# Two attention layers with 16 heads: row maxima turned by VectorE and through memory, the transposed input read from memory, scores 12 instead of 16 iterations behind the maxima, and a finer order table

## The reference, cut to what matters

```python
x = _layernorm(x + _L0_attn_ref(x, w_qkv, w_proj))                  # self: q, k rotated
x = _layernorm(x + _L0_xattn_ref(x, ctx, ctx, Wq, bq, Wk, ...))     # cross: keys, values of ctx
x = _layernorm(x + _L0_ffn_ref(x, ...))                             # windows of 128, 8 heads; MLP; twice

# self and cross, 16 heads of 16 features each, B = 8, S = 512:
attn = softmax(einsum('bhqd,bhkd->bhqk', q, k) * scale)
out = einsum('bhqk,bhkd->bhqd', attn, v) ... @ w_proj (+ bo)
```

## Time and profile before

| | |
|---|---|
| median of 3 runs | 2249.5 us (2247.09 to 2249.76) |
| span of the profiled execution | 2234.3 us, mean granted TensorE clock 0.972 |
| PE busy | 2109.7 us (94%) |
| DVE, ACT, POOL busy | 1661.7 (74%), 1501.9 (67%), 1327.5 us (59%) |
| 16-head part: first maximum to last score | 43 to 981 us |

### The profile page before, as it was taken

How to read it: one execution, slowest core, us unless ns; L and a number is a source line. 1 busy time by engine, 2 the same in 40 slices (tenths; PEclk the granted TensorE clock), 3 DMA queues, 4 the chain that set the end, 5 groups by cost and what they waited for, 6 DMA issues and landing times.

```text
span 2234.3 us, 44819 instructions
## 1 busy us (share of the span) xinstructions
PE 2109.7 (94%) x13992; PEld 1475.9 (66%) x13992; DVE 1661.7 (74%) x3987; ACT 1501.9 (67%) x3418; POOL 1327.5 (59%) x1376
## 2 busy tenths in 40 slices
PE   3899999999999999977999999899989999998998
PEld 2544444444444444346888888788878888887887
DVE  4777888777888888747888888656388888886675
ACT  2287777777888888855777777554367777775443
POOL 0344555533334444477888877454378887875775
PEclk7699999999999999999999999999999999999999
DMA  7667677665756666434545455300055554552111
GB/s 154 109 125 147 140 146 137 144 143 124 154 136 155 159 160 137 140 101 105 131 109 115 103 115 110 93 26 6 1 138 116 111 113 107 108 114 62 58 62 43
DMA packets 201337, 248.92 MB, mean 111 GB/s; under 512 B 26584, under 2 KB 119512, under 8 KB 201112
## 3 DMA queue, kind: packets, MB, share of 16 engines
q1 hardware_dynamic: 198552, 237.68, 47.7%
q0 software_dynamic: 2560, 8.39, 1.1%
HBM read 97.47 MB, written 63.44 MB: 72 GB/s over the span
## 4 chain that ended last, share of the span: by engine, by line
PE 77%; DMA 5%; POOL 5%; SPq 4%; ACT 3%; DVE 3%; issue 2%; POOLq 0%; ACTq 0%; DVEq 0%
PE PS L485 14%; PE PS L487 12%; PE PS L486 12%; PE PS L606 9%; PE PS L590 8%; PE PS L573 5%; PE PS L699 5%; PE PS L675 5%; PE PS L684 4%; DMA KS<-hs 3%; PE PS L659 2%; SPq L1496 2%; SPq L1464 1%; ACT PT L827 1%; DMA hs<-HL 1%
## 5 line engine op out<-in xcount | busy, mean ns | idle before, releaser
L1003 DVE TENSOR_REDUCE MX<-PS 128x1 f32<-128x512 f32 x1024 | 642.5, 682 | 167.1 <-PE PS L573 156.9
L827 ACT ACTIVATE PT<-PS 128x512 f32<-128x512 f32 x1024 | 546.2, 599 | 129.5 <-PE PS L590 127.6
L573 PE MATMUL PS<-KS,QS 48*128 48x512 f32 x1024 | 357.0, 454 | 43.7 <-DMA KS<-hs 33.5
L590 PE MATMUL PS<-QS,KS 50*128 50x512 f32 x1024 | 385.5, 456 | 6.4 <-ACT PT L827 6.0
L590 PEld LDWEIGHTS PS<-QS,KS 50*128 50x128 f32 x1024 | 164.9, 187 | 270.5 <-issue 212.3
L1369 POOL TENSOR_TENSOR PB<-PB,RC 128x512 f32<-128x512 f32 (+1 forms) x256 | 250.6, 999 | 48.6 <-DVE RC L1123 48.6
L606 PE MATMUL PS<-PT,VP 128*17 128x512 f32 x2048 | 273.6, 606 | 2.9 <-ACT OT L834 2.9
L890 ACT ACTIVATE PB<-PB,NMf 128x256 f32<-128x256 f32 (+1 forms) x512 | 242.6, 478 | 8.6 <-DVE NMf L1114 8.5
L573 PEld LDWEIGHTS PS<-KS,QS 48*128 48x128 f32 x1024 | 171.5, 192 | 108.0 <-issue 59.3
L1349 POOL TENSOR_TENSOR RI<-RI,mhalf 128x8 f32<-128x8 f32 x128 | 214.1, 1672 | 10.7
L1114 DVE CUSTOM_DVE_ANT_0 PB<-PS,mk 128x256 f32<-128x256 f32 (+1 forms) x512 | 175.7, 385 | 54.4 <-PE PS L675 54.2
(11 more groups left out here) (182 smaller groups left out, 5054.4 us busy)
## 6 DMA issues: line engine op xcount, KB each, us to landing
qT<-QN SPq DMA_DIRECT2D x384, 128.0 KB, 2.4
hs<-HL SPq DMA_DIRECT2D x64, 512.0 KB, 3.8
kT<-kT SPq DMA_DIRECT2D x256, 128.0 KB, 2.5
QS<-hs SPq DMA_DIRECT2D x192, 128.0 KB, 5.9
KS<-hs SPq DMA_DIRECT2D x192, 128.0 KB, 8.0
od<-OT SPq DMA_DIRECT2D x64, 256.0 KB, 5.9
OC<-od SPq DMA_DIRECT2D x32, 256.0 KB
cst<-rs SPq DMA_DIRECT2D x32, 256.0 KB
```

The costliest lines, as they stand in the source:

```text
L573: pe.matmul(PS[:, bank, :], QS[rows, s, h // 2, qt * P:(qt + 1) * P], KS[rows, s, h // 2, :], start=True, stop=True).then_inc(fills("amax" ...
L590: pe.matmul(PS[:, bank, :], KS[rows, s, pair, kt * P:(kt + 1) * P], QS[rows, s, pair, :], start=True, stop=True).then_inc(fills("score", v ...
L827: act.activation(PT[:, kt % 2, 2 * i + half], PS[:, TURNS["score", vb, g, kt, half, i][0], :], ACT.Exp).then_inc(drains("score", vb, g, kt ...
L1003: dve.tensor_reduce(MX[:, vb % 2, h // 8, qt, c:c + 1], PS[:, TURNS["amax", vb, h, qt][0], :], AX, ALU.max).then_inc(drains("amax", vb, h, ...
```

## The change

Five things change together, all in the 16-head part.
1. The maxima no longer pass TensorE and ScalarE. GpSimd splits them as before; VectorE turns 32 x 32 blocks (`maxturn`, MT<-MB, 128 x 64 in one instruction); SyncE writes them to memory (`max_out`, two transfers of 128 rows of 32 numbers) and reads them back into the score operand (`max_in`, two transfers). The sign goes into the constant rows of KS, which are -1 now.
2. For the self batches the transposed input is an array of its own in memory (x_T, made when the inputs are laid out). SyncE loads it (`load_xt`, 512 KB) into the place of the low half, ScalarE casts the high half (`xt_hi`), GpSimd makes the low half (`xt_lo`). The untransposed X is still loaded, later. `tr` is left for the cross batches only.
3. Scores run LAG = 12 iterations behind the maxima instead of 16, over the borders of the steps.
4. The tables have 96 places a step instead of 32 slots, six an iteration, and other places and lags for nearly every stage; LAST_STEP moves by 24 slots in number, which is the same distance from the end.
5. `stats` waits for the `norm` that used its buffer last, since the new order doesn't give that by itself.

```diff
+LAG = 12
 SELF_ORDER = (
-    (1, "stats", (1,), 4), (1, "ot", (3,), 2), (1, "spread", (), 3), ...
+    (0, "xt_hi", (1,), -1), (2, "mix_sum", (0, 0), -1), (3, "maxturn", (1,), 1), (3, "out_lo", (1,), 3), (4, "ot_out", (3,), 2),
...
-    for step in range(min(lags), NV + 1):
-        a, b = step, step - 1
-        at = [[] for _ in range(32)]
+    for n in range(16 * min(lags), 16 * NV + LAG + 1):
+        for half in range(2):
+            slot = 2 * n + half
             for i in range(2):
-                both = [("score", b, g, k, half, i), ("amax", a, 4 * g + 2 * i + 1 - half, k)]
+                a, b = n, n - LAG
+                both = [("score", b // 16, b // 4 % 4, b % 4, half, i), ("amax", a // 16, 4 * (a // 4 % 4) + 2 * i + 1 - half, a % 4)]
                 out += [s for s in (both if half == 0 else both[::-1]) if 0 <= s[1] < NV]
+                out += places.pop(3 * slot + i, ())
+            if half and 0 <= n - LAG - 1 < 16 * NV:
+                p = n - LAG - 1
+                out.append(("pv", p // 16, p // 4 % 4, p % 4))
+            out += places.pop(3 * slot + 2, ())
...
-            def maxtr(vb, half):
-                pe.wait_ge(sem["max_parts"], 2 * (2 * vb + half + 1))
-                bank = vacant(pe, "maxtr", vb, half)
-                for qt in range(4):
-                    m = pe.transpose(PS[0:16, bank, qt * P:(qt + 1) * P], f(MB[:, half, qt]).rearrange("p a h -> p (a h)"), ident[:])
-                m.then_inc(fills("maxtr", vb, half), 1)
-            def negmax(vb, half):
-                act.wait_ge(*filled("maxtr", vb, half))
...
+            def xt_hi(vb, kc):
+                act.wait_ge(sem["xt_in"], 16 * (vb + 1))
+                act.copy(xT[:, kc, 0], xT0[:, kc, 1]).then_inc(sem["x_hi"], 1)
+            def maxturn(vb, half):
+                dve.wait_ge(sem["max_parts"], 2 * (2 * vb + half + 1))
+                if vb:
+                    dve.wait_ge(sem["max_out"], 32 * (2 * vb + half - 1))
+                dve.transpose(MT[:, half].rearrange("p k c -> p (k c)"), f(MB[:, half]).rearrange("p k c -> p (k c)")).then_inc(sem["max_turned"], 1)
+            def xt_lo(vb, kc):
+                pool.wait_ge(sem["x_hi"], n_xhi(vb, kc))
+                pool.tensor_tensor(xT[:, kc, 1], xT0[:, kc, 1], f(xT[:, kc, 0]), ALU.subtract).then_inc(sem["x_lo"], 1)
+            def load_xt(vb):
+                if vb:
+                    sp.wait_ge(*filled("val", vb - 1, 1))
+                sp.dma_start(xT0[:, :, 1], t["x_T"][:, vb * S:(vb + 1) * S].rearrange("(k p) s -> p k s", p=P)).then_inc(sem["xt_in"], 16)
+            def max_out(vb, half):
+                sp.wait_ge(sem["max_turned"], 2 * vb + half + 1)
+                if vb:
+                    sp.wait_ge(sem["max_in"], 32 * (2 * vb + half - 1))
+                for k in range(2):
+                    v = t["ms"][half, k].rearrange("x (b j) -> b x j", b=4)
+                    sp.dma_start(v, MT[:, half, k]).then_inc(sem["max_out"], 16)
+            def max_in(vb, half):
+                sp.wait_ge(sem["max_out"], 32 * (2 * vb + half + 1))
+                if vb >= 2:
+                    sp.wait_ge(*filled("score", vb - 2, 2 * half + 1, 3, 1, 1))
+                for k in range(2):
+                    v = t["ms"][half, k].rearrange("(r c t) i -> r c (t i)", r=2, c=4)
+                    sp.dma_start(f(QS[48 + k:P:64, vb % 2, 4 * half:4 * half + 4]), v).then_inc(sem["max_in"], 16)
```

More of the change, by code:

```diff
@@ L153 @@
+            out += places.pop(3 * slot + 2, ())
+    for place in sorted(places):
+        out += places[place]
+    return out
 WINDOW_ORDER = (
@@ L595, in pv @@
                     if vb == 0:
[L596 removed]
+                        pe.wait_ge(sem["pv_zero"], 1)
                         pe.wait_ge(sem["ones_v"], 1)
```

215 lines of the change are left out of this document (103 added, 112 removed).

## The result

The changed kernel takes **2284.7 us** (median of 4 runs, 2284.3 to 2285.3) where the kernel before takes 2248.3: a ratio of **1.0173** with a 95% interval of 1.0152 to 1.0194. That is 36 us slower by the medians and 39 by the ratio, which is not formed from the medians. The forecast was 2242, with a range of 2212 to 2268. The profiled executions stand at 2283.1 us (span) against 2234.3: 48.8 us more. They are 12 more than the medians show, because the profiled execution of the kernel before was a quick one: in every other run the launch takes some 2 us more than the span of the same execution, so this one took about 2236.5, where the median is 2248.3. The 15 us between median and span, which the text before the result puts down to the launch, are mostly this.

The account below looks back on a forecast made before the run. TensorE, busy 54.3 or 54.4 of a 55.0 us steady step, was taken as the bound. Terms: -51 + 15 (start) + 20 (input) + 9 (reciprocal) = -7 against 2249.5, forecast 2242 us, range 2212 to 2268.

Parts of the forecast that it names:

- The size of the gain: 16-head part: fewer transposes, four fewer iterations and no TensorE waits for GpSimd at the maxima gain 51 us.
- the four iterations fewer: End of the 16-head part: lag 12 shortens it from 272 to 268 iterations, gaining 10.3 us.
- its 31 us: TensorE's transposes removed: 2.9 us less per self batch, 1.2 per cross batch, 31 us in all.
- the input of batch 1: Start: its load, queued on SyncE behind the first stack and X loads, lands near 62.
- C: Rival, slower: the same VectorE and ScalarE waits, each with the lower clock's price; +16, 2265 us; chance 0.27.
- the wait for the sums in steps 6 to 9: VectorE's reciprocal waits 1.9 us for the sums there, without input on GpSimd; covered, so costed at nothing.
- What one wait costs TensorE: Steps 2 to 5: VectorE's 4.5 us wait for the sums, 2.9 covered, costs TensorE 1.6, plus 0.7 low clock.
- The clock: Low TensorE clock after waits: 1 us a step beside the input's wait, 0.7 beside the sums' wait.
- The input of batches 2 to 7: Steps 0 to 5: ScalarE's cast waits 4 to 5.5 us for its load behind the stack; 20 us, bounds 0 and 33.
- The start: Step 0: batch 1's first projection comes 11 us later, plus about 4 at low clock; 15 us, bounds 3 and 20.
- D: Rival, late maxima: second-half scores wait for the maxima's way through memory; +10 to +30 us; chance 0.06.

Follow-up runs that it names:

- g1: f2 with the transposed input loaded at place 5 (before 60) and the residual at 6 (before 38): 2201.9 us, ratio 0.9793.
- g2: g1 with the context's load of the cross batches at place 34 (before 45): 2186.4 us, ratio 0.9736.
- e1: Changed kernel with the load of the sums at place 24, in front of the second stack, instead of 33: 2249.5 us, ratio 1.0023.
- e3: Changed kernel with the transposed input's load issued by ScalarE at place 79 instead of SyncE at 86: 2278.7 us, ratio 1.0188.
- f1: Changed kernel with the raw transposed input in a place of its own, loaded from place 60, residual loaded afterwards: 2277.5 us, ratio 1.0149.
- e2: Changed kernel with VectorE's reciprocal at place 44 (before 32), its write and spread also 12 places later: 2262.8 us, ratio 1.0114.
- f2: Changed kernel with both f1's early raw input and e1's sums in front of the second stack: 2232.3 us, ratio 0.9953.
- e4: Changed kernel with the start's X, identity and bias loads issued behind batch 1's transposed input: 2286.7 us, ratio 1.0224.
- f3: f2 with cross-batch places moved: reciprocal's spread 48 to 36, context 45 to 62, one heads' write 49 to 51: 2241.4 us, ratio 0.9999.

## Why the prediction was wrong

The forecast was a gain of 7 us, the profile shows a loss of 48.8: 56 us off. By stretch the forecast was too low by 36.5 us in steps 1 to 9, 9 in step 0, 8.5 in steps 10 to 14 and 2.5 behind them. In its terms:

*What held.* The size of the gain: an undisturbed cross step took 53.0 (forecast 53.8), a self step 52.5 in g1 and g2 (52.1); the four iterations fewer gave 9.0 with the transposes of the last step (forecast 10.3 + 1.2). The gain of steps 1 to 9 was even larger than its 31 us: undisturbed they take some 474 us (below), 40 less than before, as the waits for the stack went too (8.3 us of TensorE before, which the sum doesn't have). The waits and their places: the input of batch 1 landed at 61.0 (forecast near 62), in step 4 VectorE came to the reciprocal 18.9 us into the step (it begins at 299.3) and the sums landed 24.3 into it (19.1 and 23.6), and TensorE stood where the text says. C, the same waits each with the clock's price, was the nearest rival and was given 0.27; its 2265 us were still 20 too low, as it has no wait for the sums in steps 6 to 9 either.

*The step that failed: the wait for the sums in steps 6 to 9.* "...in steps 6 to 9 there is no input on GpSimd, the wait is 1.9 and covered." VectorE waited 4.9, 6.0, 5.1 and 9.3 us there, and TensorE 3.4, 5.6, 4.8 and 9.0: 22.8 of its 33 us stand in steps that were costed at nothing. The sum took GpSimd's 2.6 us for the input off the chain. At most 1.1 us of them were on it. In step 4, which has this work ahead of it, VectorE turned the maxima 3.5 us into the step after waiting 1.06 us for GpSimd; in step 7, which hasn't, it did so 3.8 us into the step without a wait, as work of its own came first. SyncE's queue in the two steps (step 7 begins at 478.8):

```profile
303.11 1.14 SPq L1529 DMA_DIRECT2D ms<-MT  x2
305.67 1.04 SPq L1537 DMA_DIRECT2D QS<-ms  x2
306.89 2.66 SPq L1511 DMA_DIRECT2D QS<-hs  x6
```
```profile
482.82 1.14 SPq L1529 DMA_DIRECT2D ms<-MT  x2
485.38 1.03 SPq L1537 DMA_DIRECT2D QS<-ms  x2
486.59 2.68 SPq L1511 DMA_DIRECT2D QS<-hs  x6
```

The stack begins 7.6 and 7.8 us into the step (forecast 8.4 and 5.8), and the sums land at 24.3 in both. In step 9 the stack begins at 11.5 only, as SyncE waits for the heads' write first.

*What one wait costs TensorE* was mis-sized by a smaller amount, 1.6 us where steps 2 to 5 show 1.2, 1.8, 3.9 and 3.2. The cover was right: from VectorE's stop to TensorE's it is 2.8 us in steps 2 to 6 (forecast 2.9), where all four banks were free and a projection stands between the maxima. In steps 7 to 9, where the banks still held two maxima and no projection stands there, it is 1.55. What the sum lacks is the way back: when the sums have landed, the reciprocal and the first reduction must pass before a bank is free, 324.84 - 323.60 = 1.24 us, in all eight steps. With it the terms close: 41.6 + 8 x 1.24 - 5 x 2.77 - 3 x 1.55 = 33.0 us. Step 7, VectorE and TensorE, for 5.96 + 1.24 - 1.55 = 5.65:

```profile
503.08 0.55 DVE L1016 RECIPROCAL RR<-RT 128x64 f32<-128x64 f32 x1 [5.96 <-DMA RT<-od]
```
```profile
504.32 0.76 PE L578 MATMUL PS<-KS,QS 48*128 48x512 f32 x1 [5.64 <-DVE MX L999]
```

e1 shows the worth of this term by a run: 35 us, though part of what the waits gave back went to others.

*The clock.* I put 1 and 0.7 us beside a wait, some 8 in all. Steps 1 to 9 are 548.5 us; at 52.5 and 53.0 they would be 6 x 52.5 + 3 x 53.0 = 474. Of the 74.5 more, 46.7 are the idle time of TensorE and 28 are left for the lower clock: 0.6 us for each us waited. This is an estimate by subtraction; the mean granted clock of the 548.5 us, 0.91, fits it: some 98 us of them stood at the lower level, idle time included. The rows for it were there before the change (a wait of 2.4 us in steps that grew by 4.5 and 6.0), and rival C used them; the forecast should have.

*The input of batches 2 to 7: the right size from a wrong cause.* Costed at 20 us, measured 12.0 of TensorE and its share of the clock. ScalarE's wait was 0.3 to 5.2 us where I had 4 to 5.5, but TensorE waited as long as ScalarE, where I took off 1.4: the cast and the first exponential, which come before a score bank is free, used up the cover. The cause I gave, the stack ahead in the queue, doesn't explain it: e3 took the queue away and the wait grew, f1 took the buffer's gate away, issued the load 26 places earlier and it was gone, while the load took the same 7.7 us in both.

*The start:* +15 forecast, less 2.9 for the transposes, and +21 measured. The first projection of batch 1 came at 64.23 (forecast 65; before 54.91, forecast 54). TensorE waited 17.9 us for it, and then 3.2 for ScalarE, where it waits for its next input, and 1.1 for the maxima's rows; before, its waits in this step were some 3 us. The mean granted clock of the step was 0.61 and not 0.66. How the rest divides between clock and waits was not tried.

*D, given 0.06,* cost the changed kernel some 8 us: steps 10 to 14 took 277.0 where five of 53.8 make 269 (12 us by the 53.0 that were measured), with waits for the maxima's rows of 1.3, 2.9 and 2.4 us in steps 11 to 13. It was the second wait in e2 and f1 (14.7 and 19.4 us of TensorE in steps 1 to 9) and the main one in f2 (27.4), where both others were gone.

Open: why e4's and f1's runs spread by 34 and 17 us, whether f3's moves cost time at all and which, and how much of f1's gain is the earlier issue by itself and how much the place ahead of the stack.

## What to carry to other kernels

What a wait costs the engine behind it is the wait, plus the work until the first buffer is free again, minus what is free when the wait begins: write down all three. A chain that loses one link is shorter only if that link was on it: look at what the next link waits for before taking it off. Give the lower clock a price of its own; here it was 0.6 us for each us waited. When a value must be read early, look for what its load must wait for before looking at its place in a queue, and put bulk loads where the DMA engines are idle, never between a small write and the read that waits for it. When several waits stand one behind the other, the run that removes the first shows only part of what it is worth.

## What the runs showed of the hardware

- A 0.5 MB load in a queue of its own took 6.6 to 10.5 us to land while another queue moved a stack, against 1.5 to 1.7 us by its bytes at 300 to 351 GB/s, the highest rates in the windows read here (an estimate). In SyncE's queue, ahead of the stack, it took 6.8 to 8.7 (f1).
- TensorE's clock fell to its lower level with an idle time of 3.91 us (value matmuls 1.91 us for eight instead of 1.05), and not behind one of 1.92 us in the same step (1.05 us behind it too). But it also fell behind idle times of 1.84 us at 261.65 (granted clock 0.50 from 262 to 274) and of 1.96 at 417.96 (0.57 from 418 to 422; the eight value matmuls took 1.91 there). The length of one wait didn't decide it.
- A small transfer pays for the bytes around it: the sums' 32 KB landed after 2.1 us alone and 5.7 to 9.8 behind a stack; the read of the maxima's 2 x 16 KB could be issued 2.6 us after their write at the beginning of step 4 (303.11, 305.67) and 8.2 us after it in the second half of step 12.
- Issuing is not free: behind the first stack and three loads of X the one issue of the identity kept SyncE 4.15 us (0.40 as the first transfer of the kernel before), and the two of the maxima took 3.45 in step 4 of f2 (1.14 in step 4 of the changed kernel).
